# Two feed-forward products of a fused attention and feed-forward block, cut in halves and put between shorter attention products on TensorE

## The reference

```
xk, xv, xr, xg = x + (shifted x - x) * maa_k, maa_v, maa_r, maa_g
r, k, v = xr @ Wr.T, xk @ Wk.T, xv @ Wv.T          32 heads of 16
g = silu(xg @ Wg.T)
per chunk of 64 tokens:
    att       = (r_c @ k_c) * w_mat                 scores, weighted
    y_c       = att @ v_c + (r_c @ state) * wb
    state     = ws * state + (k_c * wk) @ v_c
x = x + (groupnorm(y) * g) @ Wo.T
x = x + gelu(layernorm(x) @ W0.T + b0) @ W1.T + b1  hidden size 2048
```

## Time and profile before

| | us |
|---|---|
| median of 3 runs | 2120.86 |
| lowest, highest run | 2117.98, 2121.78 |
| profiled execution, its own time | 2124.26 |
| its span (first to last instruction) | 2122.5 |
| TensorE busy | 2065.3 (97%) |
| VectorE busy | 1803.2 (85%) |
| ScalarE busy | 1319.8 (62%) |
| GpSimd busy | 387.7 (18%) |
| mean granted TensorE clock | 0.994 |
| moved by the transfers | 471.60 MB, mean 222 GB/s |

### The profile page before, as it was taken

One profiled execution on the slowest core, in us unless ns is written; L12 is line 12 of the kernel. 1 busy time (PEld: TensorE's weight loads), 2 busy tenths in 40 slices (PEclk: granted clock), 3 DMA queues, 4 the chain that ended last, 5 costly groups with the idle time before them and its releaser, 6 DMA issues.

```text
span 2122.5 us, 58475 instructions
## 1 busy us (share of the span) xinstructions
PE 2065.3 (97%) x24134; PEld 1480.5 (70%) x24134; DVE 1803.2 (85%) x3623; ACT 1319.8 (62%) x2080; POOL 387.7 (18%) x329
## 2 busy tenths in 40 slices
PE   5889999999999999999999999999999999999999
PEld 5767667777666777766777776676776677777675
DVE  7778889898888889888989888898988898888771
ACT  7766556676655677655667755666765556776452
POOL 1111111211121221112122111112121212221120
PEclk8999999999999999999999999999999999999999
DMA  6967777888776788777778877777877767887677
GB/s 210 225 174 226 181 222 220 237 244 231 201 218 209 227 242 236 209 217 224 222 226 242 237 203 224 220 219 228 235 228 206 217 214 236 239 244 193 202 247 253
DMA packets 428890, 471.60 MB, mean 222 GB/s; under 512 B 259408, under 2 KB 309328, under 8 KB 428624
## 3 DMA queue, kind: packets, MB, share of 16 engines
q1 hardware_dynamic: 426992, 467.64, 76.1%
q10 hardware_dynamic: 1632, 0.21, 0.1%
HBM read 316.24 MB, written 25.17 MB: 161 GB/s over the span
## 4 chain that ended last, share of the span: by engine, by line
PE 87%; DVE 3%; SPq 3%; DMA 2%; ACT 2%; issue 1%; POOL 0%; ACTq 0%; DVEq 0%
PE F L1109 19%; PE F L1045 19%; PE B L864 11%; PE B L1017 8%; PE sc L864 8%; PE YT L896 6%; PE YT L864 4%; PE sc L926 3%; PE YT L947 2%; PE YT L990 2%; PE YT L966 2%; PE YT L1045 1%; DMA ring<-w_dram 1%; PE YT L950 1%; SPq L1982 1%
## 5 line engine op out<-in xcount | busy, mean ns | idle before, releaser
L1109 PE MATMUL F<-ring,hT 128*128 128x512 f16 x1984 | 467.8, 379 | 0.0
L1045 PE MATMUL F<-xT,ring 128*128 128x256 f16 x3840 | 451.2, 273 | 8.8 <-issue 5.2
L1045 PEld LDWEIGHTS F<-xT,ring 128*128 128x128 f16 x3840 | 370.2, 98 | 69.3 <-issue 11.9
L1109 PEld LDWEIGHTS F<-ring,hT 128*128 128x128 f16 x1984 | 186.7, 98 | 195.3
L1730 ACT ACTIVATE hT<-F,b,f_rho 128x256 f16<-128x256 f32 x480 | 243.8, 560 | 85.1 <-PE F L1045 85.0
L1926 POOL TENSOR_TENSOR Shl<-S,Shl 128x512 f16<-128x512 f32 x128 | 156.2, 1220 | 747.2 <-ACT Shl L1691 747.2
L864 PE MATMUL B<-mix,WT 128*128 128x256 f16 x2304 | 267.5, 273 | 0.0
L1691 ACT ACTIVATE Shl<-S 128x512 f16<-128x512 f32 x128 | 80.6, 630 | 286.2 <-PE YT L966 162.2
L864 PEld LDWEIGHTS B<-mix,WT 128*128 128x128 f16 x2304 | 222.8, 98 | 34.8
L267 DVE SCALAR_TENSOR_TENSOR mixf<-dx,maa,xnT 128x256 f32<-128x256 f32 x512 | 238.6, 526 | 0.1
L1316 DVE TENSOR_TENSOR att<-att 128x512 f16<-128x512 f32 x256 | 179.0, 740 | 20.0 <-ACT att L1685 19.9
(11 more groups left out here) (195 smaller groups left out, 3064.1 us busy)
## 6 DMA issues: line engine op xcount, KB each, us to landing
ring<-w_dram SPq DMA_DIRECT2D x512, 512.0 KB, 4.5
kx<-kT SPq DMA_DIRECT2D x96, 256.0 KB, 3.9
rx<-rT SPq DMA_DIRECT2D x96, 256.0 KB, 4.5
xa<-in_L_attn_x SPq DMA_DIRECT2D x32, 512.0 KB, 7.1
vbd<-vN SPq DMA_DIRECT2D x256, 64.0 KB
x<-in_L_attn_x SPq DMA_DIRECT2D x32, 512.0 KB, 6.1
out<-x SPq DMA_DIRECT2D x31, 512.0 KB, 3.8
w_dram<-ring SPq DMA_DIRECT2D x20, 256.0 KB, 3.8
```

The source lines that it names most:

```text
L1045: mm = eng.matmul(up_place(f, j)[:, i * BT:(i + 1) * BT], ring[:, use % RING, i, a * C + kk * P:a * C + (kk + 1) * P], xT[:, :, kk, :], st ...
L1109: mm = eng.matmul(F[:, t, :], hT[:, k, rows(t)], ring[:, use % RING, i, a * C:(a + 1) * C], start=(k == 0 and a == 0), stop=(k == NH - 1 a ...
```

## The change

The up product is now callable by halves (`pe_up_tile(eng, n, j, i)`); the waits that stood ahead of its matmuls (weights landed, PSUM bank free) stand ahead of half 0, and the semaphore that says "done" is raised behind half 1. In the steps in which attention and feed-forward both run (n = 2 to 31), the order of the stretch becomes: second half of G, first half of up product 6, att @ v pairs 0 to 7, second half of up product 6, att @ v pairs 8 to 15, the state's part, first half of up product 7, scores of chunk 2, second half of up product 7, output projection. The second att @ v of a step (chunks 2 and 3) stays as it was. No instruction is added or removed, and the other engines' lists are unchanged.

```diff
-    def pe_att_v(eng, n, t):
+    def pe_att_v(eng, n, t, up=False):
...
         for q in range(16):
             at = 4 * N * (q % 8)
+            if q == 8 and up:
+                pe_up_tile(eng, n, 6, 1)
             for a in range(2):
...
     def pe_up(eng, n, j):
 
+        for i in range(2):
+            pe_up_tile(eng, n, j, i)
+
+    def pe_up_tile(eng, n, j, i):
         f = n - 2
         use = UNITS * f + j
+        if i == 0:
+            pe_up_ready(eng, f, j, use)
+        for a in range(2):
+            for kk in range(G):
+                mm = eng.matmul(up_place(f, j)[:, i * BT:(i + 1) * BT],
+                                ring[:, use % RING, i, a * C + kk * P:a * C + (kk + 1) * P], xT[:, :, kk, :],
+                                start=(kk == 0 and a == 0), stop=(kk == G - 1 and a == 1))
+        if i == 1:
+            mm.then_inc(s_up, 1)
+
+    def pe_up_ready(eng, f, j, use):
+
         eng.wait_ge(s_w[use % RING], 16 * (use // RING + 1))
...
-        if ff:
+        if ff and not att_n:
             pe_up(eng, n, 6)
-        if att_n:
-            pe_att_v(eng, n, 0)
+        if ff and att_n:
+            pe_up_tile(eng, n, 6, 0)
+        if att_n:
+            pe_att_v(eng, n, 0, ff)
             pe_from_state(eng, n, 0)
+        if ff and att_n:
+            pe_up_tile(eng, n, 7, 0)
+        if att_n:
             pe_scores(eng, n, 2)
             pe_prepare(eng, n, "sc2")
-        if ff:
+        if ff and att_n:
+            pe_up_tile(eng, n, 7, 1)
+        if ff and not att_n:
             pe_up(eng, n, 7)
```

More of the change, by code:

```diff
@@ L1041, in pe_up @@
             eng.wait_ge(s_plo, 2 * PIECES)
[L1042 to L1048, removed]
     LAST_PARTS = ((0, 0, C, 2), (1, 0, C // 2, 1), (1, C // 2, C // 2, 1))
```

## The result

The changed kernel takes 2125.48 us (median of 20 runs, 2121.82 to 2128.82), beside 2121.07 us for the kernel before in the same comparison (20 runs, 2115.64 to 2126.97). The ratio is 1.0023, 95% interval 1.0015 to 1.0031: 4.9 us slower by the ratio, 4.4 by the medians. It lies inside the range. I had said 3.1 us; what was measured, 0.23%, stands just above the 0.2% at which I drew the line of "slower", and its interval (3.2 to 6.6 us) holds that line and only just misses 3.1.

A forecast was written before the change was run, and what follows sets the result against it. TensorE's own list was taken to bound the kernel. Profiled 2124.26 + 9.9 (passages) - 8.0 (pauses) = 2126.2 us; carried to ordinary runs, 2124.0 against 2120.86, slower by 3.1 us or 0.15%, range 2118.5 to 2130.

The forecast's parts named there:

- TensorE's list bounds the step: In a steady step, whatever is added to or taken from TensorE's own list changes the time one to one.
- The price of the passages: Switching between full array and parts around att @ v and scores: 0.33 us a step, 9.9 us in 30 steps.
- Pauses are late code, and a boundary wanders: Eight TensorE pauses, 8.57 us, between scores and up product 7: late code packets at boundaries wandering with a rhythm of seven.
- What each pause shrinks by: Each pause shrinks by the time it is given, 0.96 to 1.2 or 0.30 to 0.50 us; 4.7 of 8.6 saved.
- The half clock: Both half-clock stretches behind the two longest pauses go, some 1.65 us each, 3.3 us saved.
- Waits that move: Att @ v and up product 7 ask for inputs earlier; failed cover costs a few tenths each, not in the sum.
- What becomes late stays hidden: Up product 6 done some 0.7 us later, scores about 1.3, up product 7 0.33; all hidden behind other engines.
- my two readings of the 3.4 us: Profiled execution above median: fewer pauses in ordinary runs gives 2125.1 us, the profiler's own pauses 2122.8; middle 2124.0.
- R1: Rival: passages are paid, nothing is saved because packets come equally late at another boundary; 2130.8 us, chance 0.17.
- R2: Rival: all pauses go with their half-clock stretches, lateness being mostly small; 2118.9 us at most, chance 0.11.
- R3: Rival: added passages cost about nothing while the saving is as in the sum; 2114.0 us, chance 0.07.
- R4: Rival: the change does nothing, price and saving both too small; 2120.9 us, chance 0.05.

The follow-up runs named there:

- e2: The kernel before with only up product 7 split around the scores of chunk 2, up product 6 whole; ratio 0.9993 to before, -1.5 us.
- e3: The kernel before with up product 7 moved whole between the state's part and the scores of chunk 2; ratio 0.9982 to before, -3.8 us.
- e10: e7 with down product 0 moved from ahead of the scores of chunk 3 to behind them, one passage fewer; 2108.79 us, ratio 0.9958 to before.
- e9: The changed kernel with the same 19 matmuls cut in two per step as in e7; ratio 1.0017 to before, +3.6 us.
- e7: The kernel before with 19 matmuls per step cut in two from step 6, holding a block boundary within att @ v; ratio 0.9969, -6.6 us.
- e8: The kernel before padded as in e7 but from step 10, holding a block boundary behind the scores of chunk 2; ratio 1.0153, +32 us.
- e5: The kernel before loading only half of each feed-forward weight unit behind the first two steps' worth; ratio 0.9966 to before, -7.2 us.
- e1: The kernel before with only up product 6 split around pair 8 of att @ v, up product 7 whole; ratio 1.0011 to before, +2.3 us.
- e6: The changed kernel with the same half of the feed-forward weight loads left out as in e5; ratio 0.9996 to before, -0.8 us.

## Why the prediction was right, and where it wasn't

**TensorE's list bounds the step: right.** Every change of its list came out in the step's length at full size (+0.32, +0.21, +0.11, -0.11), and nothing else did.

**The price of the passages: right.** 0.33 a step was forecast, 0.32 measured; 6.36 for the stretch, 6.35 measured. The one that I could not see in the rows and put at 0.11 because the others have that size, between two kinds of parts, is confirmed as a difference: e2 and e3 add one passage in and one out, take that one away, and cost 0.11 (62.26 - 62.15); e10 puts such a one in place of an out and an in, and gains 0.11. The 0.33 had an allowance of 0.02 for cuts that begin anew; half of that was there. By the Trainium skill ("TensorEngine Tiling (Array Packing)", Key Properties) a change of tiling mode drains the engine; the price of 0.10 to 0.11 us at each passage fits that, though no run here shows the draining itself.

**Nothing covers the price: right.** e9 against e7 has the pauses out of the way and shows 10 us, give or take 3.

**Pauses are late code, and a boundary wanders: right, and now shown**, by e7 and e8, which move the boundary, and by e5, which takes traffic away and has its packets 1.13 us earlier. The "about 250 instructions" are 256, and the "2.4 to 2.7 us" from a packet's start to its use are 2.24 to 2.54 in all pauses. The Trainium skill's rule that code fetching is hidden ("Runtime: NRT & Kernel Launch", Instruction fetch mechanics) doesn't hold in this stretch: e8 lost 32 us to it.

**What each pause shrinks by: half right.** The account took the lateness of each packet in one execution and subtracted what the change gives. What it gives was right: 0.96 to 1.2 us and 0.30 to 0.50 were forecast, 1.06 to 1.09 and 0.18 to 0.58 came. The pauses followed only where the packet happened to begin nearly as before: step 9 went from 2.14 to 1.32 (forecast 1.18; packet 0.35 later), step 22 from 1.96 to 0.51 (0.76; 0.25 earlier), step 23 from 0.91 to 0.64 (0.58; 0.10 later). Step 16, which was to go from 0.36 to nothing, went to 1.38, with its packet 1.66 later; step 2 has 0.48 (forecast none; 1.43 later), step 29 has 0.56 (none; 0.72 later), and the other way those of steps 3 and 30 went altogether (1.16 and 0.52 earlier). Left are 4.89 where 3.9 was forecast. The failed step is "a pause shrinks by what it is given": it treats lateness as fixed, but e8 has 0.65 to 2.54 us at one and the same place. Only the sum over boundaries can be forecast; it was 1.0 us off, and with single misses of over 1 us in both directions that is in part luck. One premise was wrong besides: the blocks of steps 3, 16, 23 and 30 aren't entered in G or up product 6 at a place that doesn't move, but at the end of up product 6 or in att @ v, 0.37 to 0.75 us earlier in the new order.

**The half clock: right here, with less to support it than I thought.** Both stretches went (3.3 us). I had taken pauses of 1.15 and less as safe; 1.32 and 1.38 were as well, and in e8 none of 1.8 or shorter was followed by a half clock. For pauses and clock together 8.0 was forecast, and 3.7 + 3.3 = 7.0 measured.

**Waits that move: put at nothing; more in this profile, cause open.** The irregular losses of steps 2 to 30 fell by 5.1 us and not by 7.0, mainly because other waits rose by 1.7: those of up product 6 for gelus (0.82 to 1.85), G for VectorE (none to 0.89), weights (0.21 to none). The wait that I had priced at a few tenths, up product 7 for the gelu of product 5, doesn't appear at all, so its cover held. Since e7, with the order of before, has 2.1 us of gelu waits in steps 3 to 30, and e1 none, the change needn't be their cause.

**What becomes late stays hidden: right**, for the scores (1031.9 against 1032.67), and VectorE waits for them no longer than before (13.4 us in all, before 13.5). What grew is its wait for the state's part, from 66.5 to 74.1 us in 33 times, some 0.2 each; whether G's 0.89 us in step 9 comes of that isn't shown.

**From the profiled execution to the median: here the number was lost.** Of my two readings of the 3.4 us between them I took the middle. The first, fewer pauses in ordinary runs, makes the change 4.2 us slower, the second 1.9; measured are 4.9, with 3.2 to 6.6 as the interval, and that is the first. e7 points the same way: the ordinary runs of before lose 8.5 to 8.8 us to pauses, give or take 2.4, where 8.5 stood in the first reading and 11.9 in the second. A third source was left out: the time outside steps 2 to 30 isn't fixed either, 306.5 us in this execution and 302.7 to 308.1 in the ten profiles with full loads, and part of the 3.4 may lie there. Of the 8.5 to 8.8 the change saved 9.6 - 4.9 = 4.7, give or take 1.7 (5.7 forecast). With 9.9 us of price against a saving that by the first reading can't exceed 8.5, "slower by over 0.2%" needed only that less than two thirds of it went; it should have had the larger chance.

**The rivals.** R1, price paid and nothing saved: refuted as a forecast by e9, which has nothing to save and is a price of 10 us above e7, while after is only 4.9 above before. Its mechanism, packets that come later because the loads start later, isn't refuted: they began 0.29 us later in the changed kernel's profile and 0.47 later in e6 than in e5, but scattered by over 1 us. R2, all pauses go: refuted by the six that stayed, and even with it the result would have been about 2122, since ordinary runs have less to save than 11.9. R3, cheap passages: refuted by the step of 62.47. R4: refuted by both terms.

**Open.** Why e1 saved 4.0 us with one product split, where ends moved by 0.2 leave room for 1.6: its packets began 0.20 us earlier on average, which the spread from execution to execution could carry, as could the point at which the blocks are asked for, since four of the eight blocks begin earlier there too. Whether the change makes the packets later. And what, beyond its length, decides whether a pause lowers the clock, below.

## What to carry to other kernels

Small pauses put down to "issue" that come at a fixed number of instructions apart are late code: count the instructions between them before explaining them by data. What matters is how fast a block of 256 is used up; in before the eight that took 4.10 us or less paused, and in no kernel here did TensorE run dry behind one of over 5.3. The cheap cure is to let a boundary fall within the dense stretch, so that no block holds all of it (equal steps of a multiple of 256 instructions: 0.31% here). At its end, where one block holds all of it, the boundary costs 1.5%. Spreading the dense stretch out pays for every passage between tile shapes in every step to shorten one pause in four steps. And a loss that differs from execution to execution is to be priced from runs, or as a sum, never pause by pause from one profile.

## What the runs showed of the hardware that I had not expected

**The block of 256 instructions is exact**, and a pause begins at one and the same place in it, record 193 modulo 256 of TensorE's own, in every kernel here that has one. In the dense stretch 240 instructions take 2.43 us, and a block that holds it all takes 3.27, where one in e8 became usable 3.9 to 5.8 us after the block ahead of it was begun.

**Behind some long pauses the clock stays at 1.00, behind others of the same length it falls to 0.50.** Stretches of e8 behind pauses of 2.24, 1.94 and 2.46 us, and then of 1.80 and 1.97 (columns as above):

```profile
908.40:911.40 3.00, 3.00 (x15) 2.13 (x16) 2.97 (x4) 0.00 (x0) 0.41 (x1) 0.50 0.98 393
1164.30:1167.30 3.00, 3.00 (x16) 2.07 (x15) 2.25 (x3) 0.00 (x0) 0.00 (x0) 0.50 0.31 123
1294.10:1297.10 3.00, 3.00 (x13) 1.69 (x12) 1.60 (x2) 1.14 (x3) 0.00 (x0) 0.50 0.46 162
780.40:783.40 3.00, 3.00 (x23) 2.02 (x22) 2.86 (x4) 1.34 (x3) 0.21 (x1) 1.00 0.91 352
...
1930.50:1933.50 3.00, 3.00 (x24) 2.01 (x22) 2.25 (x3) 1.31 (x3) 0.00 (x0) 1.00 0.65 234
```

Four such stretches followed 23 pauses (that of step 9, ahead of the padding, among them). The shortest pause with one behind it was 1.94 us; three of 1.97 had none. So a pause of about 2 us is one that may cost its own length and another 1.65 us, or may not; its length alone doesn't tell.
